# A graph network on one core: shorter runs in the table stage's transfers, paced pieces of the first product, x normalised early, roots and last splits reordered

## The reference, cut to what matters

```python
h = relu(layernorm(x)); x = x + L0(h)   # 3 smoothing steps, mean of h and the three
h = relu(layernorm(x)); x = x + L1(h)   # weighted sum over edges / degree, two small matmuls
h = relu(layernorm(x)); x = x + L2(h)   # Chebyshev gates: two products with the weights
h = relu(layernorm(x)); x = x + L3(h)   # attention over the edges, 4 heads

# every edge sum has one of these forms, n = 3125:
segment_sum(x[src] * norm, dst, n)      # L0, norm from the in-degrees
segment_sum(x[src] * w, dst, n)         # L1, and with degree scales L2
```

## Time and profile before

| | us |
|---|---|
| three timed runs | 2566.19, 2568.54 (median), 2569.42 |
| the profiled execution, its own time | 2562.42 |
| span of its trace, first to last instruction | 2560.7 |
| first and last scatter start, POOL | 49.78, 1554.29 |
| POOL busy, DVE busy, ACT busy, PE busy | 1287.9, 1858.0, 785.6, 1212.2 |

### The profile page before, as it was taken

One profiled execution on the slowest core, in us unless ns is written; L12 is line 12 of the kernel. 1 busy time (PEld: TensorE's weight loads), 2 busy tenths in 40 slices (PEclk: granted clock), 3 DMA queues, 4 the chain that ended last, 5 costly groups with the idle time before them and its releaser, 6 DMA issues. The chain is left out here.

```text
span 2560.7 us, 40050 instructions
## 1 busy us (share of the span) xinstructions
PE 1212.2 (47%) x12261; PEld 593.6 (23%) x12261; DVE 1858.0 (73%) x3971; ACT 785.6 (31%) x1920; POOL 1287.9 (50%) x1016
## 2 busy tenths in 40 slices
PE   1111111111111111111102625899999979889987
PEld 1111111111111111111101202244344422333334
DVE  9999999999999999999841001023212589999996
ACT  0000000021332232231111112000001389999995
POOL 2688788888888888888888781000000210000001
PEclk6555555555555555555556867999999989999997
DMA  7776776667777777765656969989997753333331
GB/s 237 224 217 195 222 219 195 189 150 225 217 195 246 204 212 222 228 163 156 173 154 182 381 206 361 394 333 369 397 345 287 239 146 88 88 87 87 89 86 43
DMA packets 268041, 541.20 MB, mean 211 GB/s; under 512 B 132064, under 2 KB 140701, under 8 KB 258237
## 3 DMA queue, kind: packets, MB, share of 16 engines
q1 hardware_dynamic: 127485, 288.88, 32.3%
q10 hardware_dynamic: 26000, 245.78, 24.5%
q0 software_dynamic: 114480, 5.67, 11.0%
HBM read 371.92 MB, written 168.31 MB: 211 GB/s over the span
## 5 line engine op out<-in xcount | busy, mean ns | idle before, releaser
L1160 POOL DMA_INDIRECT table<-held x782 | 1220.2, 1560 | 331.1 <-issue 307.6
L686 DVE SCALAR_TENSOR_TENSOR resident<-resident,ring,banks 128x1280 bf16<-128x1280 f32 (+9 forms) x790 | 691.9, 941 | 0.3 <-DVE ring L672 0.3
L995 PE MATMUL banks<-ring,resident 128*128 128x6 bf16 x4345 | 128.7, 167 | 1022.3 <-DVE held L695 1022.3
L461 ACT ACTIVATE held<-held 128x128 f32<-128x128 f32 x575 | 171.8, 302 | 762.4 <-DMA weights_dram<-held 752.9
L1109 PE MATMUL banks<-ring,scaled 128*64 128x512 f32 x1250 | 315.6, 620 | 165.2 <-DVE scaled L794 81.1
L995 PEld LDWEIGHTS banks<-ring,resident 128*128 128x128 bf16 x4345 | 122.1, 104 | 1033.7 <-DVE held L695 1033.7
L1436 POOL COPY v_tile<-acc 128x64 f32 x175 | 41.3, 236 | 440.1 <-PE banks_d L1475 439.2
L678 DVE SCALAR_TENSOR_TENSOR scaled<-resident,ring,banks 128x1280 bf16<-128x1280 f32 x156 | 235.2, 1545 | 20.3 <-issue 17.6
L1208 POOL DMA_DIRECT2D parts_dram<-scaled x7 | 5.4, 778 | 449.1 <-DVE scaled L866 448.9
L1460 PE MATMUL banks_d<-held 96*128 (+2 forms) x700 | 192.7, 365 | 42.9 <-ACT att L1337 32.3
L1339 ACT ACTIVATE att<-att,shift 128x1024 f32<-128x1024 f32 (+1 forms) x175 | 208.6, 1192 | 0.0
(11 more groups left out here) (224 smaller groups left out, 1481.9 us busy)
## 6 DMA issues: line engine op xcount, KB each, us to landing
table<-acc ACTq DMA_DIRECT2D x100, 800.0 KB
held<-table ACTq DMA_DIRECT2D x24, 3200.0 KB
ring<-counts_dram SPq DMA_DIRECT2D x60, 1280.0 KB, 13.2
ring<-weights_dram SPq DMA_DIRECT2D x60, 1280.0 KB, 11.9
resident<-keys_dram SPq DMA_DIRECT2D x79, 640.0 KB
weights_dram<-held ACTq DMA_DIRECT2D x25, 1600.0 KB
counts_dram<-c_tile ACTq DMA_DIRECT2D x24, 1600.0 KB, 5.5
count<-counts_dram SPq DMA_DIRECT2D x150, 256.0 KB, 2.7
```

The source lines that it names most:

```text
L461: ins = nc.scalar.activation(w_tile[:, s], cells[:, s, :, 0], ACT.Copy, accum_out=deg_parts[:, s, bass.ds(t, 1)])
L686: ins = nc.vector.scalar_tensor_tensor(equal[b][:, OWN_AT[j]:OWN_AT[j + 1]], key_row[:, b, j * P:GE], keys[:, bass.ds(g * G + j, 1)], own_ ...
L995: nc.tensor.matmul(sums, equal[b][:, at:at + P], parts_g[:, b, j, :], start=False, stop=True, skip_group_check=True)
L1160: nc.gpsimd.indirect_dma_start(out=table, out_offset=bass.IndirectOffsetOnAxis(ap=cell[:, slot, j:j + 1], axis=0), in_=amount[:, slot, j, ...
```

## The change

- **Shorter runs.** The table's cells stand in the order (target tile, source tile, source within its tile, target), so a load reads 25 runs of 1,024 bytes for each partition. The tiles that are stored get a gap of 8 columns after each 640 (`c_both`, `w_whole`), so a store writes runs of 2,560 bytes. A zeroing quarter is written in runs of 3,200 bytes. The keys need one DVE operation on all edges less, and the mask of the low bits goes too.
- **Paced pieces.** In the first product, every third piece (number 5n + q) waits for one more landed group, from group 69 on.
- **x normalised early.** `layer_norm` is written out inside DVE's loop over the groups: the variance after 12 more groups, with some sums of weights, the rest 24 groups later. ACT takes the root of the variance behind the last zeroing, ahead of the first load.
- **Order.** DVE chooses the cells of group 1 ahead of `compare_own` of group 2. The root of the degrees stands ahead of `pass_on` of tile 19 instead of behind it. The last two tiles' weights are split by one and two wide copies, and DVE makes their row sums (`sum_weights`, which is now called twice and waits for the splits). Tile 24 comes in halves of 10 and 15 source tiles instead of 12 and 13.

```diff
+GAP = 8
+PACED_FROM = 69
+PER_GROUP = 3
-    c_tile = sb("c_tile", [P, 2, T, P], F32, c)
+    c_both = sb("c_tile", [P, 2, PIECES, PIECE * P + GAP], F32, c)
...
+    w_whole = k["held"][:, 2 * NR:3 * NR + PIECES * GAP].rearrange("p (q f) -> p q f", q=PIECES)
+    w_runs = w_whole[:, :, 0:PIECE * P]
+    zero_runs = zeros[:, 0:ZEROS // 2].unsqueeze(1).to_broadcast([P, 2, ZEROS // 2])
...
-    halves = (slice(0, PAIRS), slice(PAIRS, T))
+    halves = (slice(0, 2 * PIECE), slice(2 * PIECE, T))
...
+            def paced(prop, n, q):
+
+                number = PIECES * n + q
+                if prop == 0 and number % PER_GROUP == 0 and PACED_FROM + number // PER_GROUP <= NG:
+                    sp.wait_ge(groups_landed, PACED_FROM + number // PER_GROUP)
...
+                            paced(prop, n, q)
                             sp.dma_start(ring[:, q, 0:tiles], piece_of(dram, n, q, tiles)).then_inc(piece_landed[q], 16)
...
-                            sp.wait_ge(deg_summed, 1)
+                            sp.wait_ge(deg_summed, 2)
...
-                    act.dma_start(blocks[bass.ds(t, 1), :, cols].rearrange("a p c -> (a p) c"), zeros
+                    act.dma_start(blocks[bass.ds(t, 1), :, cols].rearrange("a p (r c) -> (a p) r c", r=2), zero_runs
                                   ).then_inc(quarter_zeroed, 16)
...
+            act.wait_ge(var_ready_a, 1)
+            nc.scalar.activation(stat[:, 2], stat[:, 1], ACT.Sqrt).then_inc(std_ready_a, 1)
+
-            whole = table[0:CELLS].rearrange("(d p f) two -> d p (f two)", d=T, p=P)
+            whole = table[0:CELLS].rearrange("(d s p c) two -> d p s (c two)", d=T, p=P, c=P)
...
-            with act.Fori(0, T // 4 - 1) as q:
+            with act.Fori(0, T // 4 - 2) as q:
                 for j in range(4):
                     pass_on(q, j)
+            for j in range(3):
+                pass_on(T // 4 - 2, j)
             act.wait_ge(turned_ready, 1)
...
             nc.scalar.activation(scale[:, DINV], clipped[:, 0], ACT.Sqrt).then_inc(root_ready, 1)
-            act.wait_ge(var_ready_a, 1)
-            nc.scalar.activation(stat[:, 2], stat[:, 1], ACT.Sqrt).then_inc(std_ready_a, 1)
-
+            pass_on(T // 4 - 2, 3)
...
             act.wait_ge(w_stored, 16 * T)
+            act.wait_ge(deg_summed, 1)
             for f, half in enumerate(halves):
                 act.wait_ge(half_landed[f], 16)
-                for s in range(half.start, half.stop):
-                    ins = nc.scalar.activation(w_tile[:, s], cells[:, s, :, 0], ACT.Copy,
-                                               accum_out=deg_parts[:, s, T - 1:T])
-                ins.then_inc(w_split, 1)
+                qs = slice(half.start // PIECE, half.stop // PIECE)
+                nc.scalar.copy(w_runs[:, qs], cells[:, half, :, 0].rearrange("p (q s) c -> p q (s c)", s=PIECE)
+                               ).then_inc(w_split, 1)
...
-            nc.vector.tensor_scalar(low_i[:], src_i[:], P - 1, None, ALU.bitwise_and)
-            link(nc.vector.tensor_tensor(keys_raw[:], src_i[:], dst_i[:], ALU.add))
-            link(nc.vector.scalar_tensor_tensor(keys_raw[:], high_i[:], float(TILE_CELLS - P), keys_raw[:],
-                                                ALU.mult, ALU.add))
-            nc.vector.scalar_tensor_tensor(keys_raw[:], low_i[:], float(NR - 1), keys_raw[:],
+            link(nc.vector.scalar_tensor_tensor(keys_raw[:], src_i[:], float(P), dst_i[:], ALU.mult, ALU.add))
+            nc.vector.scalar_tensor_tensor(keys_raw[:], high_i[:], float(TILE_CELLS - P), keys_raw[:],
                                            ALU.mult, ALU.add).then_inc(keys_ready, 1)
...
             compare_tail(2, 0)
+            choose_cells(1, 1, 0)
             compare_own(2, 0)
-            choose_cells(1, 1, 0)
-            with dve.Fori(0, ROUNDS) as o:
...
+            rounds(0, 1)
...
+            link(nc.vector.tensor_reduce(stat[:, 0], x[:], AX.X, ALU.add))
+            link(nc.vector.scalar_tensor_tensor(h[:], stat[:, 0].unsqueeze(2).to_broadcast(whole), -1.0 / D, x[:],
+                                                ALU.mult, ALU.add))
+            link(nc.vector.tensor_tensor(squares, h[:], h[:], ALU.mult))
+            link(nc.vector.tensor_reduce(stat[:, 1], squares, AX.X, ALU.add))
+            nc.vector.tensor_scalar(stat[:, 1], stat[:, 1], 1.0 / D, EPS, ALU.mult, ALU.add).then_inc(var_ready_a, 1)
...
+            rounds(1, 3)
...
+            link(nc.vector.reciprocal(stat[:, 0], stat[:, 2]))
+            link(nc.vector.scalar_tensor_tensor(h[:], h[:], 0.0, stat[:, 0].unsqueeze(2).to_broadcast(whole),
+                                                ALU.max, ALU.mult))
+            rounds(3, ROUNDS)
...
-            def sum_weights():
-
-                dve.wait_ge(w_split, T + 1)
+            def sum_weights(t, splits):
+
+                dve.wait_ge(w_split, splits)
+                ins = nc.vector.tensor_reduce(deg_parts[:, :, t].rearrange("p (q s) -> p q s", s=PIECE), w_rows, AX.X,
+                                              ALU.add)
+                if t == KEPT_OUT:
+                    ins.then_inc(deg_summed, 1)
+                    return
+                link(ins)
                 nc.vector.tensor_reduce(k["deg_out"][:], deg_parts[:], AX.X, ALU.add).then_inc(deg_summed, 1)
```

More of the change, by code:

```diff
@@ L190, in tables_and_products @@
     parts_g = take([P, 2, G, 6], BF16)
-    low_i = take(raw, I32)
     take = carver(kept_area)
@@ L505, in _ @@
             act.wait_ge(w_stored, 16 * KEPT_OUT + 16)
-            for s in range(T):
-                ins = nc.scalar.activation(w_tile[:, s], cells[:, s, :, 0], ACT.Copy,
-                                           accum_out=deg_parts[:, s, KEPT_OUT:KEPT_OUT + 1])
-            ins.then_inc(w_split, 1)
+            nc.scalar.copy(w_runs, cells[:, :, :, 0].rearrange("p (q s) c -> p q (s c)", q=PIECES)).then_inc(w_split, 1)
             act.wait_ge(w_split, KEPT_OUT + 1)
@@ L752, in next_pair, with rounds @@
                 next_group(2 * i + 2, 0, i + 1, slots[1])
+            def rounds(first, end):
+                with dve.Fori(first, end) as o:
+                    with dve.Fori(1, SLOTS // 2) as i:
+                        next_pair(SLOTS // 2 * o + i, (2 * i - 1, 2 * i))
+                    next_pair(SLOTS // 2 * (o + 1), (SLOTS - 1, 0))
             dve.wait_ge(row_landed[0], 32)
             compare_tail(2, 0)
+            choose_cells(1, 1, 0)
             compare_own(2, 0)
-            choose_cells(1, 1, 0)
@@ L837, in keep_counts @@
                     dve.wait_ge(half_landed[f], 16)
-                    nc.vector.tensor_copy(last[:, half], cells[:, half, :, 1]).then_inc(counts_kept, 1)
+                    qs = slice(half.start // PIECE, half.stop // PIECE)
+                    nc.vector.tensor_copy(c_both[:, 0, qs, 0:PIECE * P],
+                                          cells[:, half, :, 1].rearrange("p (q s) c -> p q (s c)", s=PIECE)
+                                          ).then_inc(counts_kept, 1)
             def normalise(ts, tiles, number):
@@ L1099, in _ @@
                         else:
-                            if s in (0, PAIRS) and prop == 0:
-                                pe.wait_ge(counts_kept, 2 + s // PAIRS)
+                            if prop == 0 and s in (halves[0].start, halves[1].start):
+                                pe.wait_ge(counts_kept, 2 if s == 0 else 3)
                             if s == 0 and prop == SAGE:
                                 pe.wait_ge(last_landed, 16)
-                            rows = last[:, s:s + 1]
+                            rows = last[:, q, s % PIECE].unsqueeze(1)
                         if n == 0 and s * P % BANK == 0:
```

86 lines of the change are left out of this document (40 added, 46 removed).

## The result

The changed kernel took 2586.93 us (median of 4 runs, 2585.80 to 2590.07) against 2567.82 us for the kernel before (4 runs beside it): a ratio of 1.0076, 95% interval 1.0059 to 1.0094. It is 19 us slower; 2540 was forecast, with a range up to 2560.

The account below looks back on a forecast made before the run. POOL's scatters were taken to bound the table stage; gains of 4.1 (front), 9 (zeroing), 13 (late stretch) and 2 (end) made 28 us, from 2562.4 to 2534.4, forecast as a median of 2540 us, range 2522 to 2560.

Parts of the forecast that it names:

- What bounds the kernel: Table stage: POOL's scatters, one every 1.86 us, set the time; DVE is ahead and waits 16.19 us for a slot.
- The front: Start of the table stage: first scatter 1.66 us earlier and 2.5 us less waiting up to group 2, gain 4.1 us.
- x normalised early, cost nothing: DVE's loop over groups: 11 us more work, hidden by DVE's lead of some 28 us at group 13; cost nothing.
- Shorter runs and the waits of POOL: Scatters beside transfers: each cell lets one run per busy queue pass; shorter runs gain 9 us in zeroing, 13 late.
- the 1.7 us of group 74: Loss at a late group's first scatter with pieces alone in flight, taken as evidence against turns of several runs.
- nothing is lost from 560 to 1335: Middle of the table stage: 416 scatters at 1.862 us fill 774.6 of 775 us, so no POOL time is lost.
- The late stretch: Groups 69 to 78: shorter runs and paced pieces cut POOL's loss from 25.5 to 12.5 us, gain 13.
- The sign that the prediction had named: First scatters of groups 70 to 77 still losing 3 us and more would show the forecast wrong.
- From the last scatter to the second product: End of the table stage: wide last splits save 4.4 us, row sum and later pieces cost up to 3.5; 2 gained.
- From the second product on: From the second product's start to the kernel's end: no change, 0 us.
- slower: Rival: loads in 1,024-byte runs read slowly; if a load's time doubles, 44 us against 28 gained, 2584 us; chance 0.09.
- its far end: Extreme of the slow-load rival: a 384 KB transfer at 80 GB/s, by which a load would take 42 us.

Follow-up runs that it names:

- e15: The kernel before with each piece of the first product read as two transfers with runs of 1,280 bytes instead of 2,560; 2564.57 us, 0.9987 of the kernel before.
- e3: The changed kernel with stores in runs of 12,800 bytes and zeroing in runs of 6,400 again; 2568.44 us, 1.0004 of the kernel before.
- e6: The changed kernel with only the stores in runs of 12,800 bytes again; 2569.66 us, 1.0009 of the kernel before.
- e9: The changed kernel with stores and zeroing in long runs again and no pacing, loads still in 1,024-byte runs; 2567.57 us, 1.0006 of the kernel before.

## Why the prediction was wrong, step by step

- *What bounds the kernel*: right. POOL sets the table stage, DVE still waits for slots.
- *The front*: right. The first scatter and the losses up to group 2 bring 3.8 us of the 4.1. The lead didn't last: 4.9 us at the end of group 3, 2.0 at the end of group 6, none at group 20. It went in the zeroing, at boundaries where POOL waits for landings, which is the next step but one.
- *x normalised early, cost nothing*: none of POOL's waits named DVE up to 1330 us; in the zeroing stretch POOL waited for landings (15.0 us in ten waits from 60 to 330 us, against 10.7 in eight). That this part alone costs nothing wasn't tried apart.
- *Shorter runs and the waits of POOL*: this is the step that failed. Its rule, one run for one turn, was right, though the argument for it was weak: against turns of nine runs it set the 1.7 us of group 74, and counted one cell to a turn; with a scatter's eight cells in one turn nine runs would cost 0.95 us, and group 74 could not have told. What was made of the rule was wrong. I compared each scatter's cost with the 1.862 us between two scatters, as if the mean backlog were the price. POOL only feels the backlog at a group's end. Before, the loads had 3.2 us to spare there; I took "nothing is lost from 560 to 1335" for a floor, when it was a margin. Runs that made a load last 2 us longer, and with it a store 0.9 us longer, used it up: +18.3 us instead of 0 (15 if e15's 5.0 is taken for before). The zeroing gained nothing either: +3.2 instead of -9; why its runs of half the length gained nothing wasn't taken apart as the middle was.
- *The late stretch*, the same step a second time: -7.1 instead of -13. I applied the turns to scatters against transfers and not to stores against pieces. By the same rule the critical stores lose near half their bandwidth to pieces (326 to 181 GB/s), whose runs stayed as they were. The sign that the prediction had named, 3 us and more at the first scatters of groups 70 to 77, came at three of them.
- *From the last scatter to the second product*: +6.9 instead of -2, outside the bounds (4.4 gained, 3.5 lost). The 4.4 us of the last split came; 3.3 MB of pieces in the same stretch outweighed them. I named that risk and priced it at 3.5 us at most. The cause that I named, the wait of POOL that no longer gives the store time, moved the pieces by 5.8 us; the slower store, which I hadn't counted, by 4.6 more.
- *From the second product on*: 5.8 us that I had at nothing. 1.9 lie ahead of the product's first resident piece (26.8 us after 24.9; with long stores in e3 and e6 24.5), for the last store lands later: 20.3 us after its issue at 1603.34, where 13.2 had done. The other 3.9 weren't traced, and part of them is spread between executions: from the second product on, the six kernels with short stores took 980.8 to 984.6 us (mean 982.9), the eleven with long ones 976.5 to 983.0 (mean 979.2), and the one before with its 977.1 is at the low end.
- *The rivals*: "slower" had the right side and nearly the right number, 2584, by the wrong mechanism. That number was luck. The loads of 1,024 bytes did not read slowly: 12.1 us from issue to split in quiet queues against 11.15, far from 7 us more, and e9's time shows no cost. The transfer that its far end was taken from had no such runs in the packet records either: its 384 KB went as 96 packets of 4,096 bytes. The row-pitch rule of the Trainium skill ("DMA: Bandwidth & Descriptors", "Latency and other measured facts") has half rate at pitches of 4 and 8 MiB from partition to partition, and nearly the full rate at 512 KiB. The loads here have 1,024 bytes from partition to partition and 128 KiB between the runs of one, so they don't test it; their bursts went from 9.5 to 11.5 us.
- The Trainium skill's rule in "DMA: Bandwidth & Descriptors" ("Queues, rings and completion order"), that an engine alternates by packets of several descriptors, differs from what was measured: the starts in e6 are 16 runs of the one queue and 16 of the other in turn, one for each engine. The measurement decides.

## What to carry to other kernels

A transfer's run length sets its share beside other queues: give the transfer that others wait for the longer runs, and shorten those of what is prefetched. Before lengthening a burst, measure how far it ends ahead of the point at which its neighbour waits; a stretch that loses nothing may be 2 us from losing something again and again (here 3.2 us of margin and a loss of 1.9, 2.0 and a loss of 14). When a rule of sharing is read from a trace, apply it to every pair of queues that the change touches, not only to the pair that it was made for.

## What was unexpected in the hardware

The turns are even between all three queues, the single cells of a scatter (8 bytes) included: 526 cells beside 526 and 527 runs of 2,560 bytes in 7 us. Short runs cost an engine little by themselves: mean time of a packet in the kernel before and the changed one 0.050 us for 1,024 bytes, 0.111 for 2,560, 0.142 for 3,200, 0.508 for 12,800 and 1.044 for 25,600, which is 20.5, 23.1, 22.5, 25.2 and 24.5 bytes per ns.
